# A fourth set of single row transfers per head, in place of one gather, in a graph attention and product-key attention kernel

## The chip, the cores and the metric

One NeuronCore of one Trainium2 chip. The metric is the device time of one execution in microseconds. The engines are called PE (TensorE), DVE (VectorE), ACT (ScalarE), POOL (GpSimd) and SP (SyncE); DMAs are issued by SP, ACT and POOL.

## The reference, cut to what matters

```python
def reference(x, adj, W, a, Wq_pk, pk_keys, Wq, keys_table, values_table, Wo):
    x = x + gnn(layernorm(x), adj, W, a)          # 8 batches, 1024 tokens, 128 features
    return x + ffn(layernorm(x), ...)

def ffn(x, ...):                                   # 8 heads
    q = (x @ Wq).reshape(b, n, 8, 128) * 128 ** -0.5
    kv_scores, ind = product_keys(x, Wq_pk, pk_keys)   # 16 rows of 16384 for each token and head
    k = einsum('bnhk,bnhkd->bnhd', kv_scores, keys_table[ind])
    v = einsum('bnhk,bnhkd->bnhd', kv_scores, values_table[ind])
    sim = where(causal, einsum('bihd,bjhd->bhij', q, k), neg)
    return einsum('bhij,bjhd->bhid', softmax(sim), v)... @ Wo
```

For each of 8 x 1024 tokens and each of 8 heads, 16 table rows (a key and a value side by side, 1 KB) are fetched by an index that the kernel computes, weighted and summed. That is 1,048,576 rows of 1 KB.

## The kernel before, in words

The work is cut into 64 heads (8 batches of 8 heads, numbered n = 0 to 63) of 8 units each. A unit is a tile of 128 tokens, t = 0 to 7. The table rows of a unit are 16 slots, k = 0 to 15, of 128 rows each.

**POOL** (L344 to L363) fetches them: one indirect DMA, a gather of 128 rows, for each slot, into a ring of four units (`ring`, RING = 4). Ahead of unit (n, t) it waits for the indices of that unit (`idx_ready`) and for the sum of the unit four before (`rows_summed`).

**DVE** (`head`, L1063) goes through the units in order. In unit t of head n it starts the choice of indices for unit t of head n + 1 (`choose_sets`), waits for the gathered rows of (n, t) (L1081), weights and adds slots 8 to 15 (`add_row`, L908; L917 is the first row, L920 the others) between the steps of the choice, adds PE's share of the sum (`sum_rows`, L931), and writes the indices of (n + 1, t) (`choose_rows`, L994, its last instruction L1006). So the indices of a unit are known a whole head before its rows are summed. At t = 4 the graph part writes the accumulator of the next batch (`graph_out`, L890, after the wait of L889 for the output stores of the batch before last), at t = 5 it normalises a row tile of the next batch (`graph_norm`, L903). Between batches `projection` (L822) comes in between.

**PE** weighs slots 0 to 7 (`weigh`, L646), and does the attention of the unit before. **ACT** (`head`, L515) makes the diagonals, the exponentials and the copies for it, in a fixed order written out by hand.

**The far sets.** In three units of each head, t in SETS = (3, 7, 0), slot 15 isn't gathered (L345): its 128 rows come as 128 single transfers of 1 KB each into `far`, from heads 1 on. DVE reads slot 15 from there (L912 to L915, which waits for all 128 and clears the semaphore). For this, DVE writes the 128 byte addresses (`far_at`, L1004), and a small DMA turns them into one row (`far_row`), from which the issuing engine loads addresses into registers, 32 at a time on SP, and issues the transfers (L293 on SP, L483 on ACT).

- SP serves the sets of units 3 and 7 (FAR): 256 singles a head. `far_begin(n, i)` (L273) waits for the indices and issues the small DMA; `far_fetch(n, i)` (L280) waits for it to land and for the buffer to be free (`rows_summed` of the same unit a head before), then issues four blocks of 32. `far_sets` (L298) begins set i + 1 (or set 0 of the next head) and only then fetches set i.
- ACT serves the set of unit 0 (NEAR): `near_begin` (L463) at t = 1, and `near_fetch` (L470) at the end of units 1 to 7, with 20, 20, 20, 20, 16, 16 and 16 singles.

SP also issues the load of x for the batch after next (`load`, L266, waits for L903 of the last row tile) and the 8 output stores of a batch (`stores`, L257, L264, each waits for DVE's last addition of its tile). `turn` (L306) puts the stores between the two sets of the next batch's first head.

```python
SETS = FAR + (NEAR,)
for k in range(TOPK if first or t not in SETS else FAR_ROW):
    pool.indirect_dma_start(
```

Of the kernel before, what the change touches and what calls it, by code (L numbers as in the profile page):

```python
# [11 lines left out]
U8 = mybir.dt.uint8  # L12
AX_X = mybir.AxisListType.X

P = 128
BATCH = 8
N = 1024
TILES = N // P
HEADS = 8
# [4 lines left out]
KV_BYTES = 4 * KV  # L24
# [5 lines left out]
EDGE = 256  # L30
LEAD = 2
SUMMED = UNITS - LEAD
FAR = (3, 7)
NEAR = 0
NEAR_ROWS = (0, 20, 20, 20, 20, 16, 16, 16)
SETS = FAR + (NEAR,)
FAR_ROW = TOPK - 1
LOADED = 32
BIG = 1e30
# [7 lines left out]
def gat_and_product_key_attention(nc, x, adj, W, WT, a, WqpkT, keysT, Wq, table, Wo, out):  # L47
    with ExitStack() as ctx:
# [196 lines left out]
        @block.sync  # L245
        def _(sp):
            sp.dma_start(xin[:], x[0].rearrange("(t p) d -> p t d", p=P)).then_inc(x_dma, 16)
            sp.dma_start(w_t[:], WT).then_inc(w_dma, 16)
            sp.dma_start(a_sb[:], a).then_inc(w_dma, 16)
            sp.dma_start(w_ext[:, 0:P], W).then_inc(w_dma, 16)  # L250
            sp.dma_start(mask[:].bitcast(I32), adj.rearrange("(t p) n -> p t n", p=P)).then_inc(adj_dma, 16)
            sp.dma_start(wpk_t, WqpkT).then_inc(in_dma, 16)
            sp.dma_start(keys_t, keysT).then_inc(in_dma, 16)
            sp.dma_start(wq[:], Wq.rearrange("p (h n) -> p h n", h=HEADS)).then_inc(in_dma, 16)
            sp.dma_start(wo[:], Wo.rearrange("(h p) n -> p h n", p=P)).then_inc(in_dma, 16)

            def stores(b):  # L257
                for t in range(TILES):

                    sp.wait_ge(y_added, b * HEADS * UNITS + (HEADS - 1) * UNITS + t + 1)  # L260
                    sp.sem_inc(sp_mark, 1)
                    src = acc[:, bass.ds(b % 2, 1), t * P:(t + 1) * P].rearrange("p o n -> p (o n)")
                    dst_ = out[bass.ds(b, 1), t * P:(t + 1) * P, :].rearrange("o p n -> (o p) n")
                    sp.dma_start(dst_, src).then_inc(out_dma, 16)  # L264

            def load(b):  # L266

                sp.wait_ge(g_xn, b * TILES)
                sp.sem_inc(sp_mark, 1)
                sp.dma_start(xin[:], x[bass.ds(b, 1)].rearrange("o (t p) d -> (o p) t d", p=P)) \  # L270
                    .then_inc(x_dma, 16)

            def far_begin(n, i):  # L273

                sp.wait_ge(idx_ready, n * UNITS + SETS[i] + 1)
                sp.sem_inc(sp_mark, 1)
                with nc.allow_non_contiguous_dma(reason="one table address of each token"):
                    sp.dma_start(far_row[0:1, i, :], far_at[:, i:i + 1]).then_inc(far_row_dma[i], 16)

            def far_fetch(n, i):  # L280

                sp.wait_ge(far_row_dma[i], n * 16)
                sp.sem_inc(sp_mark, 1)
                if not (isinstance(n, int) and n == 1):
                    sp.wait_ge(rows_summed, (n - 1) * UNITS + SETS[i] + 1)
                    sp.sem_inc(sp_mark, 1)
                for q in range(0, P, LOADED):
                    _, at = nc.values_load_multi_w_load_instructions(
                        far_row[0:1, i, q:q + LOADED], engines=[mybir.EngineType.SP],
                        min_val=0, max_val=(HEADS * NUM_KV - 1) * KV_BYTES,  # L290
                        skip_runtime_bounds_check_because="made of two positions below 128 and a head below 8")
                    for j in range(LOADED):
                        sp.dma_start(far[q + j:q + j + 1, i, :].bitcast(U8), table_bytes[bass.ds(at[j], KV_BYTES)]) \  # L293
                            .then_inc(far_dma[i], 16)

            last_set = len(FAR) - 1

            def far_sets(n, sets, final=False):  # L298
                for i in sets:
                    if i < last_set:  # L300
                        far_begin(n, i + 1)
                    elif not final:
                        far_begin(n + 1, 0)
                    far_fetch(n, i)

            def turn(b):  # L306
                far_sets((b + 1) * HEADS, range(0, last_set))
                stores(b)
                far_sets((b + 1) * HEADS, range(last_set, last_set + 1))

            load(1)
            far_begin(1, last_set + 1)
            far_begin(1, 0)
            far_fetch(1, last_set + 1)
            with sp.Fori(1, HEADS) as h:
                far_sets(h, range(len(FAR)))
            with sp.Fori(0, BATCH - 2) as b:
                load(b + 2)
                turn(b)
                with sp.Fori(1, HEADS) as h:  # L320
                    far_sets((b + 1) * HEADS + h, range(len(FAR)))
            turn(BATCH - 2)
            with sp.Fori(1, HEADS - 1) as h:
                far_sets((BATCH - 1) * HEADS + h, range(len(FAR)))
            far_sets(BATCH * HEADS - 1, range(len(FAR)), True)
            stores(BATCH - 1)
            sp.wait_ge(out_dma, BATCH * TILES * 16)

# [38 lines left out]
        def _(act):  # L367
# [99 lines left out]
                with nc.allow_non_contiguous_dma(reason="one table address of each token"):  # L467
                    act.dma_start(far_row[0:1, near, :], far_at[:, near:near + 1]).then_inc(far_row_dma[near], 16)

            def near_fetch(n, part):  # L470

                if NEAR_ROWS[part - 1] == 0:
                    act.wait_ge(far_row_dma[near], n * 16)
                    act.sem_inc(act_mark, 1)
                    act.wait_ge(rows_summed, (n - 1) * UNITS + NEAR + 1)
                    act.sem_inc(act_mark, 1)
                q = sum(NEAR_ROWS[:part])
                _, at = nc.values_load_multi_w_load_instructions(
                    far_row[0:1, near, q:q + NEAR_ROWS[part]], engines=[mybir.EngineType.Activation],
                    min_val=0, max_val=(HEADS * NUM_KV - 1) * KV_BYTES,  # L480
                    skip_runtime_bounds_check_because="made of two positions below 128 and a head below 8")
                for j in range(NEAR_ROWS[part]):
                    act.dma_start(far[q + j:q + j + 1, near, :].bitcast(U8), table_bytes[bass.ds(at[j], KV_BYTES)]) \  # L483
                        .then_inc(far_dma[near], 16)

            act.wait_ge(aux_mm, 1)
            nc.scalar.copy(w_ext[:, P:P + 1], wh_ps[:, 0:1]).then_inc(aux_copied, 1)
# [27 lines left out]
            def head(b, h, n, graph, ahead, first=False):  # L515
                if ahead and not first:
                    query_weights((h + 1) % HEADS, n + 1)
                for t in range(UNITS):
                    g = n + TILES
                    behind = (n, t - 1) if t else (n - 1, UNITS - 1)  # L520
                    if graph and t == 4:
                        graph_elu(g)
                    if graph and t == 5:
                        graph_sqrt(g)
                    if t or not first:
                        attend_exp(*behind)
                    if graph and t == 6:
                        graph_keep(b + 1, h, g)
                    if ahead and t == 1 and not first:
                        near_begin(n + 1)  # L530
                    if ahead:
                        t1 = (t + 1) % UNITS
                        n1 = n + 1 + (t + 1) // UNITS
                        choose_begin(n1 // HEADS if graph else BATCH - 1, n1 * UNITS + t1, t1)
                    if t or not first:
                        attend_turned(*behind)
                    if ahead:
                        choose_softmax((n + 1) * UNITS + t)
                    attend_begin(n, t)
                    if t < UNITS - 1:  # L540
                        if not first or t + 1 > SUMMED:
                            diagonals(n, t + 1)
                    elif ahead:
                        diagonals(n + 1, 0)
                    if t or not first:
                        attend_out(*behind)
                    if ahead:
                        choose_query((n + 1) * UNITS + t, t)
                    if graph and t == 1:
                        graph_exp(g)  # L550
                    if graph and t == 2:
                        graph_copy(g)
                    if ahead and t >= 1 and not first:
                        near_fetch(n + 1, t)
                if not ahead:
                    attend_exp(n, UNITS - 1)
                    attend_turned(n, UNITS - 1)
                    attend_out(n, UNITS - 1)
# [593 lines left out]
```

## Time and profile before

| What | us |
|---|---|
| median of 3 runs | 15304.31 (15302.25 to 15309.95) |
| profiled execution, first to last instruction of the core (the span) | 10159.7 |
| POOL busy in it | 7625.7 (75%) |
| DVE busy | 6962.0 (69%) |
| PE busy | 5615.2 (55%) |
| ACT busy | 3117.0 (31%) |

The page gives the profiled execution's span and no other time of it. The median of the runs is 5144.6 us above that span. Busy time does not count instructions that issue DMAs on SP and ACT, register and semaphore instructions. In the timeline views SPq and ACTq are the sequencers of SP and ACT, where DMAs are issued.

### The profile page before, as it was taken

The numbers are of one execution on the slowest core, as the hardware profiler recorded it, in microseconds if no ns is written. First come the engines' busy times: TensorE is split into PE (matmuls) and PEld (weight loads), VectorE is DVE, ScalarE is ACT, GpSimd is POOL, SyncE is SP. The second block draws the span as 40 slices with busy tenths as digits, with TensorE's granted clock in tenths as the row PEclk, the third lists the DMA queues.
The fourth block names the chain that finished last, engine by engine and source line by source line (L and its number), as shares of the span: only waits on it lengthen the run. The fifth ranks groups of instructions, "written<-read, shape, count | busy, mean of one in ns | idle before, by whom it ended". The sixth has DMA issues, their size and how long they took to land.

```text
span 10159.7 us, 173542 instructions
## 1 busy us (share of the span) xinstructions
PE 5615.2 (55%) x23108; PEld 4511.4 (44%) x23108; DVE 6962.0 (69%) x42780; ACT 3117.0 (31%) x9770; POOL 7625.7 (75%) x8020
## 2 busy tenths in 40 slices
PE   5655555555555555555555555555555555555555
PEld 4544444444444444444444444444444444444444
DVE  8866667666666667666776666766667676666663
ACT  4333233332333333333333233333333333322222
POOL 5777777777777777777777777777777777777776
PEclk7777777777777777777777777777777777777777
DMA  3333333333333333333333333333333333333333
GB/s 109 104 108 108 108 112 108 108 108 108 112 108 107 108 108 112 108 108 108 108 112 108 108 108 108 112 108 108 107 110 110 108 108 108 108 110 108 108 108 99
DMA packets 481297, 1099.25 MB, mean 108 GB/s; under 512 B 180864, under 2 KB 222720, under 8 KB 479968
## 3 DMA queue, kind: packets, MB, share of 16 engines
q0 software_dynamic: 384144, 1049.48, 36.1%
q1 hardware_dynamic: 71152, 31.60, 1.2%
q10 hardware_dynamic: 24800, 8.19, 0.4%
q14 instruction: 1184, 9.70, 0.3%
q8 instruction: 17, 0.28, 0.0%
HBM read 1084.36 MB, written 4.19 MB: 107 GB/s over the span
## 4 chain that ended last, share of the span: by engine, by line
POOL 73%; issue 24%; DVE 2%; PE 1%; POOLq 0%; DMA 0%; ACT 0%; ACTq 0%; SPq 0%; DVEq 0%
POOL ring L346 73%; DVE hot L998 0%; PE ps_o L709 0%; DMA wo<-in_Wo 0%; DVE ps_v L920 0%; POOLq L362 0%; PE ps_p L595 0%; POOLq L360 0%; DMA ring<-in_table,idx 0%; PE ps_p L599 0%; ACTq L483 0%; PE ps_s L681 0%; DVE nmax L1049 0%; PE ps_w L656 0%; DVE edge L849 0%
## 5 line engine op out<-in xcount | busy, mean ns | idle before, releaser
L346 POOL DMA_INDIRECT ring<-in_table,idx x8003 | 7624.1, 953 | 2507.7 <-issue 2440.8
L656 PE MATMUL ps_w<-ring,diag 128*128 128x256 f32 x8192 | 1996.2, 400 | 9.7 <-DMA ring<-in_table,idx 9.6
L700 PE MATMUL ps_p<-ident,prob 128*128 128x128 f32 x2304 | 548.8, 390 | 2576.1 <-ACT prob L446 2568.1
L656 PEld LDWEIGHTS ps_w<-ring,diag 128*128 128x128 f32 x8192 | 1630.3, 205 | 244.8 <-issue 12.7
L917 DVE TENSOR_SCALAR ps_v<-ring,wgt 128x256 f32<-128x256 f32 x512 | 248.7, 486 | 2147.8 <-DMA ring<-in_table,idx 2147.8
L998 DVE SCALAR_TENSOR_TENSOR hot<-rank,posf,cand 128x54 f32<-128x54 f32 x8192 | 1655.4, 270 | 0.3
L700 PEld LDWEIGHTS ps_p<-ident,prob 128*128 128x128 f32 x2304 | 371.4, 194 | 2769.7 <-ACT prob L446 1734.0
L920 DVE SCALAR_TENSOR_TENSOR ps_v<-ring,wgt,ps_v 128x256 f32<-128x256 f32 x3072 | 1478.1, 481 | 19.6
L437 ACT ACTIVATE diag<-ident,wgt 128x128 f32<-128x128 f32 x4096 | 1251.9, 391 | 0.0
L668 PE MATMUL ps_t<-ident,kv 128*128 128x128 f32 x512 | 234.4, 458 | 1642.4 <-DVE kv L931 1642.4
L709 PEld LDWEIGHTS ps_o<-probT,kv 128*128 128x128 f32 x4608 | 1040.8, 318 | 145.9 <-ACT probT L454 69.9
L446 ACT ACTIVATE prob<-ps_s,nmax 128x128 f32<-128x128 f32 (+7 forms) x512 | 378.1, 738 | 2324.8 <-issue 1777.3
L709 PE MATMUL ps_o<-probT,kv 128*128 128x128 f32 x4608 | 1035.4, 404 | 43.7 <-ACT probT L454 43.7
L668 PEld LDWEIGHTS ps_t<-ident,kv 128*128 128x128 f32 x512 | 92.1, 180 | 1803.4 <-DVE kv L931 1802.7
L681 PE MATMUL ps_s<-kT,qT 128*128 128x512 f32 (+3 forms) x1536 | 784.6, 630 | 1.6 <-issue 1.2
L998 DVE DVE_READ_ACCUMULATOR hot<-rank,posf,cand 128x1 f32 x8192 | 651.3, 79 | 0.0
L634 PE MATMUL ps_v<-pk,xt 128*128 (+1 forms) x1026 | 545.6, 632 | 13.6 <-ACT xt L412 7.5
L931 DVE TENSOR_TENSOR kv<-part,ps_w 128x256 f32<-128x256 f32 x512 | 215.7, 421 | 453.9 <-PE ps_o L709 407.0
L454 ACT COPY probT<-ps_p 128x512 f32<-128x512 f32 (+3 forms) x768 | 351.7, 480 | 414.2 <-PE ps_p L700 412.3
L681 PEld LDWEIGHTS ps_s<-kT,qT 128*128 128x128 f32 x1536 | 366.7, 271 | 194.9 <-issue 188.2
L441 ACT COPY kT<-ps_t 128x128 f32<-128x128 f32 x512 | 135.9, 265 | 977.6 <-PE ps_t L668 977.4
L941 DVE MAX8 side<-ps_v 128x8 f32<-128x128 f32 x1024 | 253.6, 289 | 212.2 <-issue 181.0
(119 smaller groups left out, 8053.9 us busy)
## 6 DMA issues: line engine op xcount, KB each, us to landing
far<-in_table SPq DMA_DIRECT2D x16256, 1.0 KB
ring<-in_table,idx POOLq DMA_INDIRECT x8003
far<-in_table ACTq DMA_DIRECT2D x7936, 1.0 KB
xin<-in_x SPq DMA_DIRECT2D x8, 512.0 KB, 4.6
mask<-in_adj SPq DMA_DIRECT2D x1, 4096.0 KB, 14.6
out_x<-acc SPq DMA_DIRECT2D x64, 64.0 KB
far_row<-far_at SPq DMA_DIRECT2D x127, 0.5 KB
far_row<-far_at ACTq DMA_DIRECT2D x62, 0.5 KB
```

The lines of the kernel that those rows point to most:

```text
L346: pool.indirect_dma_start(out=ring[:, t % RING, k, :], out_offset=None, in_=table, in_offset=bass.IndirectOffsetOnAxis(ap=idx[:, t, k:k + ...
L437: nc.scalar.mul(diag[:, k, :], ident[:], wgt[:, t, k:k + 1]).then_inc(diag_ready, 1)
L446: nc.scalar.activation(prob[:, 0:cols], ps_s[:, 0:cols], ACT.Exp, bias=nmax[:, 0:1], accum_out=psum_row[:, 0:1]).then_inc(p_exp, 1)
L454: nc.scalar.copy(probT[:, c * 512:c * 512 + m], ps_p[:, c, 0:m]).then_inc(p_copied, 1)
L634: nc.tensor.matmul(ps_sim, xt[:, t % 2, :], pk[:, bass.ds(h, 1), :, :].rearrange("p o s n -> p (o s n)"), start=True, stop=True).then_inc( ...
L656: ins = nc.tensor.matmul(pw_ps, diag[:, k, :], ring[:, t % RING, k, :], start=(k == 0), stop=(k == PE_ROWS - 1))
L668: nc.tensor.transpose(ps_t[:, 0, :], kv[:, t, 0:P], ident[:]).then_inc(k_tp, 1)
L681: nc.tensor.matmul(ps_s[:, c * 512:c * 512 + m], q, kT[:, c * 512:c * 512 + m], start=True, stop=(c < HALVES[t] - 1))
L700: ins = nc.tensor.transpose(ps_p[:, c, (j % 4) * P:(j % 4 + 1) * P], prob[:, j * P:(j + 1) * P], ident[:])
L709: ins = nc.tensor.matmul(oT_ps, kv[:, j, P:KV], probT[:, j * P:(j + 1) * P], start=(j == 0), stop=(j == t))
L920: row_sum[0] = step(nc.vector.scalar_tensor_tensor(out=part[:] if k == TOPK - 1 else ps_part, in0=rows, scalar=w, in1=ps_part, op0=ALU.mul ...
L998: c = step(nc.vector.scalar_tensor_tensor(out=hot[:, k, :], in0=rank[:], scalar=posf[:, k:k + 1], in1=cand[:, 1, :], op0=ALU.is_equal, op1 ...
```

## The change

A fourth set is added. The units with a set become SETS = (1, 3, 6, 0), so POOL gathers 124 slots a head in place of 125. SP issues the sets of units 3 and 6 and rows 32 to 127 of the set of unit 1 (352 singles a head); ACT issues the set of unit 0 and rows 0 to 31 of the set of unit 1 (160 singles a head). ACT's parts at the end of units 1 to 7 become 28, 28, 24, 24, 24 (set of unit 0), 16 and 16 (set of unit 1).

`far_fetch` now issues the `far_begin` of the next set ahead of its own last block of 32, and not ahead of all four. The stores of a batch move there too, ahead of the last block of the third set of the next batch's first head. Before the first head, SP fetches the set of unit 0 and begins that of unit 1 within it.

```diff
-FAR = (3, 7)
+FAR = (1, 3, 6)
 NEAR = 0
-NEAR_ROWS = (0, 20, 20, 20, 20, 16, 16, 16)
+SHARED = 0
 SETS = FAR + (NEAR,)
+ACT_ROWS = (32, 0, 0, P)
+NEAR_PLAN = {1: ((3, 0, 28),), 2: ((3, 28, 56),), 3: ((3, 56, 80),), 4: ((3, 80, 104),), 5: ((3, 104, 128),),
+             6: ((0, 0, 16),), 7: ((0, 16, 32),)}
...
-            def far_fetch(n, i):
+            def far_fetch(n, i, first, after_begin=None, follow=None):
...
-                for q in range(0, P, LOADED):
+                for q in range(first, P, LOADED):
+                    if q == P - LOADED:
+                        if follow is not None:
+                            far_begin(*follow)
+                        if after_begin is not None:
+                            stores(after_begin)
...
-            def far_sets(n, sets, final=False):
-                for i in sets:
+            def far_sets(n, final=False, stored=None):
+                for i in range(len(FAR)):
                     if i < last_set:
-                        far_begin(n, i + 1)
-                    elif not final:
-                        far_begin(n + 1, 0)
-                    far_fetch(n, i)
-
-            def turn(b):
-                far_sets((b + 1) * HEADS, range(0, last_set))
-                stores(b)
-                far_sets((b + 1) * HEADS, range(last_set, last_set + 1))
+                        far_fetch(n, i, ACT_ROWS[i], follow=(n, i + 1))
+                    else:
+                        far_fetch(n, i, ACT_ROWS[i], stored, None if final else (n + 1, 0))
 
             load(1)
             far_begin(1, last_set + 1)
-            far_begin(1, 0)
-            far_fetch(1, last_set + 1)
+            far_fetch(1, last_set + 1, 0, follow=(1, 0))
...
             with sp.Fori(0, BATCH - 2) as b:
                 load(b + 2)
-                turn(b)
+                far_sets((b + 1) * HEADS, stored=b)
...
-            def near_fetch(n, part):
+            def near_fetch(n, i, first, stop):
...
-                if NEAR_ROWS[part - 1] == 0:
-                    act.wait_ge(far_row_dma[near], n * 16)
+                if first == 0:
+                    act.wait_ge(far_row_dma[i], n * 16)
                     act.sem_inc(act_mark, 1)
-                    act.wait_ge(rows_summed, (n - 1) * UNITS + NEAR + 1)
-                    act.sem_inc(act_mark, 1)
+                    if not (isinstance(n, int) and n == 1):
+                        act.wait_ge(rows_summed, (n - 1) * UNITS + SETS[i] + 1)
+                        act.sem_inc(act_mark, 1)
...
-                    if ahead and t >= 1 and not first:
-                        near_fetch(n + 1, t)
+                    if ahead:
+                        for i, lo, hi in NEAR_PLAN.get(t, ()):
+                            if i == SHARED or not first:
+                                near_fetch(n + 1, i, lo, hi)
```

## Rows read from the trace of the kernel before

**Rows 1.** The page: span, and busy time, share and instructions of each engine.

```profile
span 10159.7 us, 173542 instructions
PE 5615.2 (55%) x23108; PEld 4511.4 (44%) x23108; DVE 6962.0 (69%) x42780; ACT 3117.0 (31%) x9770; POOL 7625.7 (75%) x8020
```

**Rows 2.** The page: the chain that ended last, shares by line (first line of two).

```profile
POOL 73%; issue 24%; DVE 2%; PE 1%; POOLq 0%; DMA 0%; ACT 0%; ACTq 0%; SPq 0%; DVEq 0%
```

**Rows 3.** Waits of POOL, whole span: us in total, times, longest.

```profile
POOL ring L346 <- issue: 2440.8, 7998, 0.3
POOL ring L346 <- DVE idx L1006: 55.8, 1, 55.8
POOL ring L346 <- DVE kv L931: 11.1, 4, 10.2
```

**Rows 4.** The page's costliest group: busy us, mean ns, idle before.

```profile
L346 POOL DMA_INDIRECT ring<-in_table,idx x8003 | 7624.1, 953 | 2507.7 <-issue 2440.8
```

**Rows 5.** Waits of all engines, those of DVE on rows: us, times, longest.

```profile
DVE ps_v L917 <- DMA ring<-in_table,idx: 2147.8, 420, 10.4
...
DVE part L920 <- DMA far<-in_table: 9.0, 2, 7.0
```

**Rows 6.** Timeline of SP at a batch boundary: start us, length us, what.

```profile
5036.72 0.48 SPq L278 DMA_DIRECT2D far_row<-far_at  x1
5039.66 48.33 SPq L293 DMA_DIRECT2D far<-in_table  x128
5091.09 0.41 SPq L270 DMA_DIRECT2D xin<-in_x  x1
...
5168.39 5.88 SPq L264 DMA_DIRECT2D out_x<-acc  x8
```

**Rows 7.** Waits of SP, whole span: us in total, times, longest.

```profile
SPq L276 <- DVE idx L1006: 3170.9, 126, 32.4
```

**Rows 8.** Timeline of DVE, ten moments; L1006 ends the index choice of a unit.

```profile
5076.76 0.35 DVE L903 TENSOR_SCALAR xn<-x,gmv,row 128x128 f32<-128x128 f32 x1
...
5151.96 0.42 DVE L931 TENSOR_TENSOR kv<-part,ps_w 128x256 f32<-128x256 f32 x1 [8.92 <-PE ps_o L709]
...
5172.86 0.26 DVE L1006 CAST idx<-idxf 128x16 uint32<-128x16 f32 x1
...
5214.89 0.26 DVE L890 TENSOR_SCALAR acc<-x 128x128 f32 x1
...
5254.66 0.17 DVE L1006 CAST idx<-idxf 128x16 uint32<-128x16 f32 x1
...
5316.46 0.27 DVE L1006 CAST idx<-idxf 128x16 uint32<-128x16 f32 x1
...
5350.86 0.15 DVE L1004 TENSOR_SCALAR far_at<-idxf 128x1 uint32<-128x1 f32 x1
5350.93 0.17 DVE L1006 CAST idx<-idxf 128x16 uint32<-128x16 f32 x1
...
5412.30 0.17 DVE L1006 CAST idx<-idxf 128x16 uint32<-128x16 f32 x1
...
5473.70 0.19 DVE L1006 CAST idx<-idxf 128x16 uint32<-128x16 f32 x1
```

**Rows 9.** Timeline of ACT, end of unit 1 of head 33 and after it.

```profile
5318.84 6.50 ACTq L483 DMA_DIRECT2D far<-in_table  x20
5325.38 0.47 ACT L446 ACTIVATE prob<-ps_s,nmax 128x256 f32<-128x256 f32 x1 [7.06 <-issue]
```

**Rows 10.** Timeline of POOL: the first gather of unit 4 of head 32.

```profile
5183.46 0.95 POOL L346 DMA_INDIRECT ring<-in_table,idx  x1 [0.31 <-issue]
```

**Rows 11.** Timeline of SP at the start: the first set 0 and set 3.

```profile
240.72 49.04 SPq L293 DMA_DIRECT2D far<-in_table  x128
...
293.05 48.56 SPq L293 DMA_DIRECT2D far<-in_table  x128
```

**Rows 12.** Timeline of POOL: its one long stall behind DVE, head 1, unit 2.

```profile
269.69 0.97 POOL L346 DMA_INDIRECT ring<-in_table,idx  x1 [10.15 <-DVE kv L931]
```

More of the change, by code:

```diff
@@ L296, in _ @@
             last_set = len(FAR) - 1
-            def far_sets(n, sets, final=False):
-                for i in sets:
+            def far_sets(n, final=False, stored=None):
+                for i in range(len(FAR)):
                     if i < last_set:
-                        far_begin(n, i + 1)
-                    elif not final:
-                        far_begin(n + 1, 0)
-                    far_fetch(n, i)
-            def turn(b):
-                far_sets((b + 1) * HEADS, range(0, last_set))
-                stores(b)
-                far_sets((b + 1) * HEADS, range(last_set, last_set + 1))
+                        far_fetch(n, i, ACT_ROWS[i], follow=(n, i + 1))
+                    else:
+                        far_fetch(n, i, ACT_ROWS[i], stored, None if final else (n + 1, 0))
             load(1)
             far_begin(1, last_set + 1)
-            far_begin(1, 0)
-            far_fetch(1, last_set + 1)
+            far_fetch(1, last_set + 1, 0, follow=(1, 0))
             with sp.Fori(1, HEADS) as h:
-                far_sets(h, range(len(FAR)))
+                far_sets(h)
             with sp.Fori(0, BATCH - 2) as b:
                 load(b + 2)
-                turn(b)
+                far_sets((b + 1) * HEADS, stored=b)
                 with sp.Fori(1, HEADS) as h:
-                    far_sets((b + 1) * HEADS + h, range(len(FAR)))
-            turn(BATCH - 2)
+                    far_sets((b + 1) * HEADS + h)
+            far_sets((BATCH - 1) * HEADS, stored=BATCH - 2)
             with sp.Fori(1, HEADS - 1) as h:
-                far_sets((BATCH - 1) * HEADS + h, range(len(FAR)))
-            far_sets(BATCH * HEADS - 1, range(len(FAR)), True)
+                far_sets((BATCH - 1) * HEADS + h)
+            far_sets(BATCH * HEADS - 1, True)
             stores(BATCH - 1)
@@ L468, in near_begin @@
                     act.dma_start(far_row[0:1, near, :], far_at[:, near:near + 1]).then_inc(far_row_dma[near], 16)
-            def near_fetch(n, part):
-                if NEAR_ROWS[part - 1] == 0:
-                    act.wait_ge(far_row_dma[near], n * 16)
+            def near_fetch(n, i, first, stop):
+                if first == 0:
+                    act.wait_ge(far_row_dma[i], n * 16)
                     act.sem_inc(act_mark, 1)
-                    act.wait_ge(rows_summed, (n - 1) * UNITS + NEAR + 1)
-                    act.sem_inc(act_mark, 1)
-                q = sum(NEAR_ROWS[:part])
+                    if not (isinstance(n, int) and n == 1):
+                        act.wait_ge(rows_summed, (n - 1) * UNITS + SETS[i] + 1)
+                        act.sem_inc(act_mark, 1)
                 _, at = nc.values_load_multi_w_load_instructions(
-                    far_row[0:1, near, q:q + NEAR_ROWS[part]], engines=[mybir.EngineType.Activation],
+                    far_row[0:1, i, first:stop], engines=[mybir.EngineType.Activation],
                     min_val=0, max_val=(HEADS * NUM_KV - 1) * KV_BYTES,
                     skip_runtime_bounds_check_because="made of two positions below 128 and a head below 8")
-                for j in range(NEAR_ROWS[part]):
-                    act.dma_start(far[q + j:q + j + 1, near, :].bitcast(U8), table_bytes[bass.ds(at[j], KV_BYTES)]) \
-                        .then_inc(far_dma[near], 16)
+                for j in range(first, stop):
+                    act.dma_start(far[j:j + 1, i, :].bitcast(U8), table_bytes[bass.ds(at[j - first], KV_BYTES)]) \
+                        .then_inc(far_dma[i], 16)
             act.wait_ge(aux_mm, 1)
```

## The prediction

> **What bounds the kernel now.** I read first who ends last. In the chain of the whole span POOL's gathers and the "issue" time between them are 97% [rows 2]. Busy shares alone would not say this: POOL is at 75% and DVE at 69% [rows 1]. The waits of POOL settle it [rows 3]. Nearly all its idle time, 2440.8 us in 7998 pieces of 0.3 us, is the gap from one gather to the next, on which nothing but POOL itself works. For indices it waits once, at the start (55.8 us), and for DVE to free the ring 11.1 us in all. So POOL runs from gather to gather without a stop, and a gather costs its busy time and the gap: (7624.1 + 2440.8) / 8003 = 1.258 us [rows 4]. 8003 of them are 10065 of the 10159.7 us.
>
> Everything else has to be no more than in time. DVE waits 2147.8 us for gathered rows, in 420 of 512 units, and only 9.0 us, at the start, for single transfers [rows 5]. SP stands 3170.9 us waiting for indices [rows 7], 50 us of a head's 157.
>
> **The change, part by part.** *Removed:* one gather in each of heads 1 to 63, 125 to 124, 63 in all: 8003 become 7940. Each is worth 1.258 us as long as POOL never waits. One is lost again: in head 1 POOL stands 10.15 us at unit 2, until DVE has summed unit 6 of head 0 [rows 12]. It comes there one gather earlier now and waits that much longer. That leaves 62 x 1.258 = 78.0 us.
>
> *SP: 256 to 352 singles a head.* A set of 128 takes 48.33 us from first to last issue and 2.46 us ahead of it (from the end of L278 to the first single: landing of the small DMA, loading of addresses) [rows 6], so 12.7 us for a block of 32. Eleven blocks are 140 us, three begins at 0.48 us make 141. A head takes 157.2 us now (5316.46 to 5473.70, unit 1 to unit 1 [rows 8]) and 156.0 then. SP is filled to 91%, and 15 us are left. Its waits for indices, with index 1 of head n + 1 ready at time 0: the last block of the set of unit 6 goes out to 13; three blocks of set 1 to 51, whose last needs index 3, ready at 34.5; set 3 has three blocks out at 90, then waits for index 6 until 95.8, and ends at 109; set 6 has three blocks out at 147 and waits for the next index 1 at 156. DVE reads these sets at about 156, 190 and 252: over 80 us to spare for each. In steady state this costs nothing, and what hides it is that a set is asked for a head ahead.
>
> *The batch boundary,* where `load` now holds set 1 and not set 3. `load` waits for L903 at 5076.76 [rows 8]. From 5077.5, SP needs ten blocks without a stop until its last block of set 6: 5077.5 + 127 + 1 = 5206. Set 1 is out at 5116, set 3 at 5167; unit 1 of head 32 ends at 5172.86. Then come the stores, 5.88 us [rows 6], to 5212, and the last block to 5225, against 5254.66 for unit 6. All arrive. The tight one is L890 at 5214.89, which waits until the stores of two batches before the one it writes have landed. They are issued at 5168 to 5174 before and to about 5212 then, so 3 us are left for landing, and I count a DVE stall of 0 to 5 us at each of six boundaries. DVE lags most here, yet the sum of unit 0 of head 32 at 5151.96 is 31 us ahead of the gather that needs it, at 5183.46 [rows 8, 10]. The stall stands in front of units where DVE waits for rows anyway. Counted at 0, upper end 6 x 5 = 30 us.
>
> *The start.* SP's first set comes 30 us earlier, since its begin of the second set no longer waits ahead of it (240.72 becomes about 210 [rows 11]). Then follow without a stop four blocks of set 0, three of set 1 and four of set 3, so set 3 ends near 210 + 11 x 12.7 = 350, where it ended at 341.6 (293.05 + 48.56), and set 6 near 400. DVE may wait some 10 us for each in head 1 and up to 20 us in head 2; POOL is three units, over 55 us, from needing those sums. Zero, upper end 20 us.
>
> *ACT: 128 to 160 singles a head.* 20 of them take 6.50 us, and the `prob` behind them stood 7.06 us [rows 9], 0.353 us each. Units 1 and 2 take 28, so 2.8 us more, units 3 and 4 four more, unit 5 eight more; what moves into units 6 and 7 is as many as before. That is 11.3 us a head. Queued behind it are `prob` and PE's transposes of the unit before, then the scores that DVE's maximum needs. DVE's cover is its own wait for rows, 2147.8 / 64 = 34 us a head [rows 5]. Zero on the path. ACT also waits at unit 6 for the small DMA of set 1, which SP issues at index 1, five units earlier; at a boundary at 5194 against about 5255. No stop.
>
> *DVE:* one more address column a head, 0.15 us [rows 8], under the same cover. *POOL's own rate:* the same transfers leave its queue and go to two others. Nothing in the rows prices a slower gather beside more singles; by the gap that is constant at 0.30 us while SP and ACT issue, I take no change, and 0.2% of the gathers' 10065 us (20 us) to either side.
>
> **Sum.** Span 10159.7 - 78.0 = 10081.7 us. The median of the runs is 5144.6 us above the span, which no row covers; the three runs lie within 7.7 us of each other, so I take it as a constant around the kernel: 15304.3 - 78.0 = 15226.3 us, 0.51% less. About 0.2% (31 us) is what a measurement of this kernel can tell from no change.
>
> The Trainium skill speaks against this change (DMA: Bandwidth & Descriptors, Rules for kernel authors): many small transfers should be made into one large one, since under 64 KB one pays mostly overhead. The trace agrees on the overhead, 48.33 us of issue for what a gather does in 1.258. By that rule taken as a cost on the path the sum would be 63 x (48 - 1.3) = some 2900 us slower; by the rows it lies on SP and ACT, which do not end last.
>
> **Rivals.** *(a) The part outside the span scales.* If the timed executions are longer throughout by 15304.3 / 10159.7 = 1.506, each gather is worth 1.89 us and the result is 15304.3 - 117.5 = 15187. For it: a constant of 5 ms is odd. Against: nothing in the trace shows a slower gather. 11%. The Trainium skill (Runtime: NRT & Kernel Launch, The ~15us preamble/postamble breakdown) puts 9 to 15 us around a kernel; no run shows that here, and it would leave the 5 ms inside the execution, which speaks for (a).
>
> *(b) Partly given back:* boundary stores and the start reach POOL, up to 30 + 20 us: 15240 to 15276. Against: 31 us and 55 us of ring in hand. 9%.
>
> *(c) Slower: SP becomes the bound.* Its place is the eleven blocks a head. At over 156.0 / 11 = 14.2 us a block SP falls behind, and above 14.3 us the kernel is slower than before, 12% more than the 12.7 us of now. If a single cost what an output store costs to issue (5.88 / 8 = 0.74 us, the nearest dearer row [rows 6]) in place of 0.38, the head would be 352 x 0.74 = 259 us and the kernel 6 ms slower; a third of that step, 0.12 us on a single, is 352 x 0.12 = 42 us, a head of 183 us and 63 x 26 = 1640 us slower: 16940. Against: the three sets shown, at the start and in the middle, took 48.33, 48.56 and 49.04 us [rows 6, 11], which differ by 1.5%. 8%.
>
> *(d) The gather stays, or something else cancels it:* within 31 us of before. Slots are left out by `t in SETS`, so it does go. 4%.
>
> **How the numbers follow.** Forecast 68%, (a) 11%, (b) 9%, (c) 8%, (d) 4%. The range takes in the forecast with its 20 us on the gather's rate, (a) and (b): 15180 to 15275; outside are (c) and (d), 12%, and the ends of the others. Faster by over 0.2%: 68 + 11 + 8 = 87%. Within: 5%. Slower: 8%.
>
> **What would show it.** Right: 7940 gathers at 1.258 us, POOL still waiting for no one but in head 1, a span near 10082, SP's waits for indices down from 50 to some 15 us a head, DVE's wait for singles still near zero. Wrong: POOL waiting for L931 in every head (c), or at every eighth (b); mean gather or gap longer; a time that falls by 1.5 times the fall of the span (a).

## The result, and the profile after

| | before | after | after / before (95%) |
|---|---|---|---|
| median of 4 runs, us | 15306.77 | 17009.96 | 1.1113 (1.11 to 1.1126) |
| span of the profiled execution, us | 10159.7 | 17004.4 | |

The kernel after is 11% slower; 15226 was forecast, with 15180 to 15275 as the range. The profiled execution after took 17006.56 us, 2.2 us more than its span. So nothing of 5144 us lies around this kernel, and the profile of before shows an execution that is unlike the timed ones. The page of the kernel after, against [rows 1, 2]:

```profile
span 17004.4 us, 190424 instructions
PE 5905.6 (35%) x23108; PEld 4760.9 (28%) x23108; DVE 7154.1 (42%) x42844; ACT 3064.3 (18%) x9770; POOL 7557.6 (44%) x7957
...
SPq 62%; issue 37%; DVE 1%; another core or an unknown queue 0%; PE 0%; ACT 0%; DMA 0%; DVEq 0%; ACTq 0%
SPq L301 52%; SPq L296 8%; SPq L281 1%; SPq L267 0%; DVE hot L1001 0%; DMA wo<-in_Wo 0%; DVE ps_v L923 0%; SPq L289 0%; SPq L288 0%; SPq L286 0%; ACT L398 0%; DVE edge L852 0%; DVE edge L865 0%; SPq L278 0%
...
L347 POOL DMA_INDIRECT ring<-in_table,idx x7940 | 7556.1, 952 | 9371.7 <-issue 6604.2
```

The reader is to see who took POOL's place. The engines are busy for about as long as before, within a span that is two thirds longer, and the chain is SP's queue: L301 issues the singles, L296 loads their addresses. A gather still takes 952 ns (953 in [rows 4]). POOL's idle time is now pauses between the gathers of one unit and the next: 510 of them last over 1 us, 7050 us together, and the profile of before has one of 10 us. The mean granted clock of TensorE is lower too, 0.650 against 0.728, but PE is busy only 290 us longer in a span that is 6845 us longer, and DVE's additions of gathered rows (L923, L920 before) keep their 481 ns, so a slower clock isn't what costs. The waits of POOL, and those of DVE for singles, in the kernel after, against [rows 3, 5]:

```profile
POOL ring L347 <- issue: 6604.2, 7743, 40.1
POOL ring L347 <- DVE kv L934: 2647.3, 187, 44.2
...
DVE part L923 <- DMA far<-in_table: 1454.3, 121, 49.0
```

The timeline of SP in the kernel after, one head, against [rows 6]:

```profile
8022.60 67.72 SPq L301 DMA_DIRECT2D far<-in_table  x96
8090.53 0.51 SPq L281 DMA_DIRECT2D far_row<-far_at  x1
8093.53 91.43 SPq L301 DMA_DIRECT2D far<-in_table  x128
8185.16 0.49 SPq L281 DMA_DIRECT2D far_row<-far_at  x1
8188.12 94.95 SPq L301 DMA_DIRECT2D far<-in_table  x128
8283.29 0.49 SPq L281 DMA_DIRECT2D far_row<-far_at  x1
```

128 singles take 91 to 95 us where they took 48.33, and a head 263.6 us (8022.60 to 8286.23, where the next head's first set starts). SP never waits for an index but once. What stretches its issue is seen when the issues are held against POOL's. The instructions of L301 in the kernel after, first in 18 us in which POOL gathers without a pause, then in 7 us in which it rests (count; ns min/median/max):

```profile
L301 SPq DMA_DIRECT2D far<-in_table x14: 3/14/702, 8365.6 to 8383.4; - x14
L301 SPq MOVE far<-in_table x13: 4/15/700, 8366.3 to 8382.6; - x13
```

```profile
L301 SPq MOVE far<-in_table x22: 13/29/29, 8386.9 to 8393.6; - x22
L301 SPq DMA_DIRECT2D far<-in_table x22: 218/225/321, 8386.9 to 8393.7; - x22
```

The timeline of POOL for the same stretch of the kernel after:

```profile
8364.23 0.99 POOL L347 DMA_INDIRECT ring<-in_table,idx  x1 [18.97 <-issue]
8365.52 0.95 POOL L347 DMA_INDIRECT ring<-in_table,idx  x1 [0.30 <-issue]
...
8383.32 0.94 POOL L347 DMA_INDIRECT ring<-in_table,idx  x1 [0.30 <-issue]
8393.97 1.00 POOL L347 DMA_INDIRECT ring<-in_table,idx  x1 [9.71 <-issue]
```

14 singles in 18 us, 1.3 us each, against 0.32 us each while POOL rests. Some DMA instructions stretch to 0.7 us, and so do some plain register MOVEs; the others are recorded as short as 3 ns, so the pace says more here than the length of one instruction. Over the whole trace SP's singles start 1.20 us apart on average while POOL gathers and 0.43 us apart in its pauses, the loading of addresses between the blocks included (pairs less than 5 us apart, a pause being one of over 1 us). In the profile of before it is 0.38 us while POOL gathers. In the first profile of the kernel before SP issued at full pace while POOL gathered without a pause [rows 3, 6].

### The profile page after: what moved, and what is told of

Its sections match the earlier page's. It is cut to its first block, busy times and chain, and to the rows that moved or that the text cites. A ratio compares the mean times of both kernels' runs of the same rounds, so it can differ in the third digit from the quotient of the medians.

```text
span 17004.4 us, 190424 instructions
## 1 busy us (share of the span) xinstructions
PE 5905.6 (35%) x23108; PEld 4760.9 (28%) x23108; DVE 7154.1 (42%) x42844; ACT 3064.3 (18%) x9770; POOL 7557.6 (44%) x7957
## 4 chain that ended last, share of the span: by engine, by line
SPq 62%; issue 37%; DVE 1%; another core or an unknown queue 0%; PE 0%; ACT 0%; DMA 0%; DVEq 0%; ACTq 0%
SPq L301 52%; SPq L296 8%; SPq L281 1%; SPq L267 0%; DVE hot L1001 0%; DMA wo<-in_Wo 0%; DVE ps_v L923 0%; SPq L289 0%; SPq L288 0%; SPq L286 0%; ACT L398 0%; DVE edge L852 0%; DVE edge L865 0%; SPq L278 0%
## 5 line engine op out<-in xcount | busy, mean ns | idle before, releaser
L659 PE MATMUL ps_w<-ring,diag 128*128 128x256 f32 x8192 | 2313.9, 446 | 6.9 <-issue 6.8
L659 PEld LDWEIGHTS ps_w<-ring,diag 128*128 128x128 f32 x8192 | 1866.8, 234 | 337.2 <-issue 18.5
L923 DVE SCALAR_TENSOR_TENSOR ps_v<-ring,wgt,ps_v 128x256 f32<-128x256 f32 x3072 | 1476.4, 481 | 444.4 <-remote 276.1
L1063 DVE SCALAR_TENSOR_TENSOR acc<-ps_o,rz,acc 128x128 f32 (+1 forms) x512 | 179.4, 350 | 1742.1 <-remote 1271.9
L718 PE MATMUL ps_o<-wo,oT 128*128 (+1 forms) x1024 | 308.7, 394 | 1439.5 <-ACT oT L459 795.5
L923 DVE SCALAR_TENSOR_TENSOR part<-far,wgt,ps_v 128x256 f32<-128x256 f32 x252 | 121.0, 480 | 1454.4 <-DMA far<-in_table 1454.3
L718 PEld LDWEIGHTS ps_o<-wo,oT 128*128 128x128 f32 x1024 | 205.1, 250 | 1505.2 <-ACT oT L459 768.4
L1016 DVE TENSOR_SCALAR wgt<-ew,ewsum 128x16 f32<-128x16 f32 x512 | 127.9, 250 | 1170.8 <-remote 899.0
L955 DVE MATCH_VALUE_LOAD sidx<-side,left 128x8 f32 x1024 | 88.0, 86 | 1182.4 <-remote 839.2
L419 ACT ACTIVATE qT<-ps_t 128x128 f32<-128x128 f32 x512 | 142.2, 278 | 2263.3 <-remote 1922.4
```

Of the source, the lines that this page charges most:

```text
L659: ins = nc.tensor.matmul(pw_ps, diag[:, k, :], ring[:, t % RING, k, :], start=(k == 0), stop=(k == PE_ROWS - 1))
L718: nc.tensor.matmul(y_ps, oT[:], wo[:, bass.ds(h, 1), :].rearrange("p o n -> p (o n)"), start=True, stop=True).then_inc(y_mm, 1)
L923: row_sum[0] = step(nc.vector.scalar_tensor_tensor(out=part[:] if k == TOPK - 1 else ps_part, in0=rows, scalar=w, in1=ps_part, op0=ALU.mul ...
```

## The experiments

Each set of runs has the kernel before timed on the same chip. The ratios below are against it.

**First set: is the time in the kernel, and what do single sets do?** e1 is the kernel before. e2 has no singles:

```diff
-FAR = (3, 7)
+FAR = ()
-SETS = FAR + (NEAR,)
+SETS = ()
```

with the calls of `far_begin`, `far_fetch`, `near_begin` and `near_fetch` left out. e3 keeps the set of unit 0 (`FAR = ()`), e4 those of units 3 and 7 (`SETS = FAR`).

> The kernel before, unchanged, profiled again, with 256 single transfers a head on SP and 128 on ACT. Theory S (stalled issue): in the kernel after, SP and ACT issue singles at 0.32 us while POOL gathers nothing, and in steps of 0.7, 1.4 and 2.1 us while it gathers; the timed runs of the kernel before were in that state too and its first profile was not. Then this profile shows a span near 15300 us, POOL's gaps no longer at 0.30 us, and SPq L293 issues of 0.70 us. Rival C (a constant outside the span): span near 10160 us and a time near 15305 us.

> All 16 slots of all units are gathered, no single transfers: 64 x 128 = 8192 gathers. Theory S: nothing stalls, POOL runs from gather to gather at 1.258 us, 8192 x 1.258 = 10306, span and time near 10390 us, a third less than the kernel before. Rival C: span 10400, time 15540 us. Rival T (gathers themselves are slower in timed runs, 1.9 us each): time near 15650 us.

> Only the set of unit 0 stays, 128 singles a head on ACT (127 gathers removed to 127 a head, 8129 in all). Theory S with the singles' number deciding: each single that meets a gather costs its engine about 1.7 us; 128 of them on ACT are over 200 us a head, so some 11000 to 14000 us. If both engines issuing at once is what starts the stalls: near 10310 us.

> Only the sets of units 3 and 7 stay, 256 singles a head on SP (126 gathers a head, 8066 in all). If the stall needs only one engine's singles beside gathers: SP is as slow as in the kernel before, 15000 us or a little less. If it takes SP and ACT at once: near 10230 us.

Measured: the kernel before 10138.26 us, e1 10137.73 with a span of 10135.2, e2 10364.53 (ratio 1.0223, 1.0194 to 1.0253), e3 10288.34 (1.0148), e4 10207.27 (1.0067). Neither theory's line for e1 came out: the span is near 10160 and the time is too. This chip runs the kernel before a third faster than the chip of the first comparison. I call such a chip quick and the other kind stalling. The constant outside the span is dead. Here each set of singles is a gain: 76 us from e2 to e3, 150 more from e3 to the kernel before with two more sets, or 75 to 76 a set, and 69 us from e4 to the kernel before; 63 gathers at 1.258 us would be 79. e3 and e4 met no stall and say nothing of it. For e1 on this chip, L293:

```profile
L293 SPq MOVE far<-in_table x16256: 29/29/42, 241.9 to 10067.6; - x199
L293 SPq DMA_DIRECT2D far<-in_table x16256: 224/225/457, 242.0 to 10067.6; - x199
```

**Second set: the kernel after again (e5), and without singles (e6).** The kernels are unchanged.

> The kernel after, unchanged. The kernel before took 15307 us in the first comparison and 10138 us in the runs of e1, so the stall depends on where or when a program runs, and a comparison is only good within one set of runs. Theory S: where the kernel before is at 10138 us, the singles go out at 0.32 us each beside gathers, and the kernel after is 62 gathers of 1.258 us faster, 10060 us; where before is at 15307, after is at 17010. Rival N (the larger number of singles is what starts the stall): after is near 17000 us in either case.

> The kernel without singles (8192 gathers), unchanged from e2, where it took 10364.5 us. Theory S: it has nothing that can stall, so it takes 10365 us also where the kernel before takes 15307 us; then it is the fastest of the three there. If the chip state slows the gathers too: far over 10400 us there.

Measured: before 15566.48, e5 17358.16 (1.1151, 1.1133 to 1.117), e6 13617.13 (0.8747, 0.8729 to 0.8764). A stalling chip. The kernel after repeats its 11%. The kernel without singles is the fastest of the three here, but my 10365 us for it was wrong by 3250: the stall isn't of singles alone. The page of e6, then its waits of DVE:

```profile
DVE 57%; another core or an unknown queue 26%; issue 9%; PE 6%; ACT 1%; DVEq 1%; DMA 0%; ACTq 0%; SPq 0%
...
L336 POOL DMA_INDIRECT ring<-in_table,idx x8192 | 7789.0, 951 | 5780.6 <-issue 4407.8
```

```profile
DVE top L962 <- remote: 1563.9, 413, 5.8
...
DVE side L941 <- DVE sidx L938: 106.3, 182, 1.1
```

Gathers take 951 ns here too (949 in e2). But DVE, between two of its own instructions (L938 and L941, the second waits for the first's semaphore), stands 0.58 us on average in 182 cases, and 1563.9 us ahead of L962; in e2 neither wait exists. SP's few register MOVEs last up to 728 ns in e6 and at most 42 in e2. So other engines are held up without any singles, DVE becomes the one that ends last (57% of the chain), and POOL pauses over 1 us 509 times, each time ahead of the first gather of a unit.

**Third set: which part of the change?** e7 is the kernel before, e8 the kernel after. e9 is the kernel after without its fourth set, so that only the new order of begins, stores and ACT's parts is left (125 gathers, 256 and 128 singles):

```diff
-FAR = (1, 3, 6)
+FAR = (3, 6)
-ACT_ROWS = (32, 0, 0, P)
+ACT_ROWS = (0, 0, P)
```

with ACT's parts at units 1 to 5 alone. e10 moves 64 more singles from SP to ACT:

```diff
-ACT_ROWS = (32, 0, 0, P)
+ACT_ROWS = (96, 0, 0, P)
-             6: ((0, 0, 16),), 7: ((0, 16, 32),)}
+             6: ((0, 0, 32),), 7: ((0, 32, 64), (0, 64, 96))}
```

> The kernel before, once more, for its profile beside the next three on one chip. Two conditions have been seen: one in which it takes 10138 us (call it quick) and one in which it takes 15307 to 15566 (stalling). Theory S for the stalling one: while POOL gathers, about half of the singles on SP last 0.7 us in place of 0.23, and none while POOL rests; POOL gathers at 1.258 us in both and rests 80 us a head. Rival D: the DMA queues are full, then packets start later after their issue than the 1.08 us of the quick profile.

> The kernel after. In the quick condition theory S says that the sum of the prediction holds there: 62 gathers of 1.258 us, 78 us faster than the kernel before, 10060 us, POOL not waiting. In the stalling condition 11% slower than before, as in the first comparison and in e5. Rival N (352 singles are too many for SP in any condition): slower than 10138 in the quick one too.

> The kernel after without its fourth set: sets of units 3, 6 and 0, 256 singles on SP and 128 on ACT, 125 gathers a head, with the new order of begins, stores and ACT parts. Quick: 10138 us, the same as before within 0.1%. Stalling: theory S says that the 128 added singles are what costs, so it is at or below the kernel before, 15300 to 15600 (the new order takes 5 us of exposed waits a head off SP, so up to 2% less). Rival O (the new order of waits is what costs): near 17000 to 17360, as after.

> The kernel after with 64 more singles of the fourth set on ACT: SP 288 and ACT 224 a head (ACT at units 6 and 7). Quick: POOL does not wait, 10060 us as after. Stalling: if SP's issue is the bound (62% of the chain of the kernel after is SP's queue), 64 singles less at 0.75 us shorten a head by up to 48 us, so 14300 to 16000 us; rival L (the sum of all engines' stalls binds, not SP's): within 2% of after, or slower.

Measured, a quick chip again: before 10158.63, e7 10158.33, **e8 10082.49 (0.9925, 0.9908 to 0.9941), 76.1 us faster**, e9 10155.22 (0.9996), e10 10988.29 (1.0817). Rival N is out: 352 singles a head are not too many for SP where nothing stalls. The profile of e8 is the one that the prediction described, by its page, the waits of POOL and of DVE on the sets, and the waits of SP:

```profile
span 10083.2 us, 190424 instructions
...
POOL 72%; issue 24%; DVE 1%; PE 1%; ACTq 1%; POOLq 0%; DMA 0%; ACT 0%; SPq 0%; DVEq 0%
...
L347 POOL DMA_INDIRECT ring<-in_table,idx x7940 | 7560.0, 952 | 2494.7 <-issue 2424.5
```

```profile
POOL ring L347 <- DVE kv L934: 13.4, 2, 13.1
...
DVE part L923 <- DMA far<-in_table: 6.3, 2, 4.1
```

```profile
SPq L272 <- DVE xn L906: 473.1, 7, 170.3
SPq L279 <- DVE idx L1009: 248.3, 33, 28.4
SPq L264 <- DVE acc L1063: 120.9, 7, 20.2
```

The expectation for e10 missed by 900 us. The chain of e10 by its page, then waits of PE, ACT and DVE:

```profile
ACTq 41%; PE 28%; issue 16%; DVE 10%; ACT 4%; POOL 1%; DMA 0%; DVEq 0%; SPq 0%; POOLq 0%
```

```profile
PE ps_p L703 <- ACT prob L447: 4845.2, 491, 28.0
...
ACT L430 <- issue: 1175.8, 42, 28.4
...
DVE kv L934 <- PE ps_o L712: 1789.1, 63, 31.4
```

ACT stands up to 28.4 us ahead of the first instruction of a head, behind 64 singles in one burst at unit 7. PE's attention waits for it, and DVE's sum of the next head's first unit, which must wait for the last output sum (63 times, once a head), for PE. With 224 singles ACT is the bound even where nothing stalls.

**Fourth set: the same four questions where it stalls.** e11 is the kernel before, e12 the kernel of e9, e13 that of e10, e14 that of e4.

> The kernel before, for its profile in the stalling condition if the chip shows it (time 15300 to 15570 us; in the quick one 10140 to 10160, as in e1 and e7, and nothing new). Theory S, stalling: SP's queue ends last or nearly so, 40 to 55% of the singles that SP issues while POOL gathers last over 0.6 us, none while POOL rests, POOL rests some 80 us a head.

> The kernel after without its fourth set (256 singles on SP, 128 on ACT, 125 gathers), new order kept. Quick: 10155 us as in e9. Stalling: theory S (the number of singles costs) puts it at or up to 2% below the kernel before; rival O (the new order costs) at 17000 us or more.

> The kernel after with 64 more singles on ACT (SP 288, ACT 224). Quick: 10988 us as in e10, where ACT is what is late. Stalling: if SP's queue is the bound of the kernel after, 64 x 0.75 = 48 us a head less on SP, as far as ACT lets it: 14300 to 16500 us. If not SP's queue but the stalls of all engines bind: 17000 us or more.

> Sets of units 3 and 7 on SP alone (256 singles a head on SP, none on ACT). Quick: 10207 us as in e4. Stalling: without singles it was 13617 us (e6) and with all three sets 15566. If singles on SP stall by POOL's gathers alone: SP needs as long as in the kernel before, 15000 to 15570 us. If they stall by ACT's singles beside them: near 13600 us.

Measured, a stalling chip: before 15286.68, e11 15287.45, e12 15191.89 (0.9932, 0.9916 to 0.9948), e13 16902.16 (1.1055, 1.1022 to 1.1088), e14 14606.92 (0.9554, 0.9526 to 0.9581). Three things follow. The new order is not what costs, it is a gain of 0.7% here and nothing on a quick chip: rival O is out and the fourth set's singles are the cause. The stalls don't need both queues: with singles on SP alone the chain of e14 is SP's queue. But e14 met neither of its expectations (15000 to 15570, or near 13600): it lies between them, and ACT's 128 singles cost as well. And e13 missed its 14300 to 16500: with 64 singles fewer SP is no longer the bound, but ACT is next, as in e10. For e11, L293 over the whole span; then the first lines of the chains of e11, e12, e14 and e13, in this order:

```profile
L293 SPq MOVE far<-in_table x16256: 2/29/1479, 331.0 to 15285.9; - x199
L293 SPq DMA_DIRECT2D far<-in_table x16256: 3/225/1482, 331.1 to 15285.9; - x199
```

```profile
issue 24%; another core or an unknown queue 23%; DVE 16%; SPq 11%; ACTq 11%; PE 8%; ACT 6%; DVEq 0%; DMA 0%
```

```profile
another core or an unknown queue 30%; issue 21%; ACTq 16%; DVE 14%; PE 10%; ACT 9%; DVEq 0%; DMA 0%; SPq 0%
```

```profile
SPq 56%; issue 42%; DVE 1%; PE 0%; another core or an unknown queue 0%; ACT 0%; DMA 0%; DVEq 0%; ACTq 0%
```

```profile
another core or an unknown queue 28%; ACTq 27%; issue 20%; ACT 9%; DVE 9%; PE 7%; DVEq 0%; DMA 0%; SPq 0%
```

The kernel before, when it is timed on such a chip, is no longer POOL's. Its chain goes through all engines; SP still waits 261.3 us for indices. Theory S had SP's queue last or nearly so in e11, and that was wrong: it is 11% of the chain. Of its other signs the 84 us a head of POOL's pauses came out; of SP's singles 35% last over 0.6 us while POOL gathers, where 40 to 55% were expected, and 4% while it rests. A register MOVE of SP lasts up to 1479 ns in e11 and at most 42 in e1, the same program. Rival D, full DMA queues, has little for it: the packet of a single starts 0.84 us (median) after its issue in e11, sooner than the 1.08 us of e7, and at most 4 are issued and not started (5 in e7). These delays are rough in e11: with singles and packets matched in order, 22% of the packets start before the recorded start of their own issue (none in e7), so on such a chip part of the instructions are recorded late. The pace doesn't hang on those records: while POOL gathers, the packets themselves start 1.11 us apart on average in e11 and 0.38 in e7.

**Fifth set: does SP's count decide?** e15 puts ACT's 32 singles of the fourth set on SP (`ACT_ROWS = (0, 0, 0, P)`), e16 is the kernel after.

> The kernel after with its fourth set whole on SP: SP 384 singles a head, ACT 128. Quick condition: twelve blocks at 12.9 us and the waits for indices fill 156 us or pass it, so SP is the bound or just not: 10080 to 10500 us. Stalling: if SP's queue bounds the kernel after, 32 singles more at 0.75 us are 24 us a head, some 1500 us slower than after, 18500 us; as only a single issued while POOL rests is added (0.33 us), at least 10 us a head, 650 us slower. If the stalls of all engines bind and not SP, within 2% of the kernel after.

> The kernel after, as the reference of e15 on the same chip. Theory S: 0.9925 of the kernel before if that takes 10140 to 10160 us, 1.11 if that takes 15290 to 15570.

Measured, a stalling chip: before 15519.93, e15 18146.54 (1.1695, 1.1656 to 1.1733), e16 17276.09 (1.1134, 1.1097 to 1.117). The chain of e15:

```profile
SPq 63%; issue 36%; DVE 1%; another core or an unknown queue 0%; PE 0%; ACT 0%; DMA 0%; DVEq 0%; ACTq 0%
```

32 singles more on SP, taken from ACT, are 870 us, over 63 heads 13.8 us a head or 0.43 us a single. That lies between the 10 and the 24 us a head expected, and the rival, within 2% of the kernel after, is out. From e14 (256 on SP) to e16 (352) it is (1.1134 - 0.9554) x 15520 / 63 / 96 = 0.41 us a single, over two chips. In these three kernels the chain is SP's queue, and SP's count sets the time. In the others it doesn't: e12 has the 256 singles of e14 on SP and 128 more on ACT, takes 585 us longer, and SP isn't in its chain. So that both steps have the same price assumes that ACT's singles cost nothing once SP ends last, which no run shows by itself. The price is less than the mean of 0.75 us a single in the kernel after, since the added time is time in which POOL rests: its pauses over 1 us are 7333.5 us in e16 and 8201.1 in e15, 867.6 of the 870 us, and in these pauses the singles of e16 start 0.43 us apart.

All sets together, by kind of chip (the kernel before = 1):

| kernel | singles a head, SP + ACT | quick chips | stalling chips |
|---|---|---|---|
| no singles | 0 | 1.0223 | 0.8747 |
| sets of units 3, 7 | 256 + 0 | 1.0067 | 0.9554 |
| before | 256 + 128 | 1 (10138, 10159 us) | 1 (15287 to 15566 us) |
| new order, no fourth set | 256 + 128 | 0.9996 | 0.9932 |
| after | 352 + 160 | 0.9925 | 1.1113, 1.1151, 1.1134 |
| 64 more on ACT | 288 + 224 | 1.0817 | 1.1055 |
| all on SP | 384 + 128 | not run | 1.1695 |

No kernel tried is the best on both. The new order without the fourth set is nowhere slower than before.

## Why the prediction was wrong

- **The step that failed: "I take it as a constant around the kernel".** The sum had a term of 5144.6 us that no row covered, and carried it over. In each profiled execution since, the time is about 2 us over the span: 17006.56 and 17004.4, 10364.92 and 10363.1. The profile of before was of an execution of the quick kind, the runs beside it of the stalling kind. So every cover was read in the wrong condition, and a gap of a third of the time was itself the sign of it. Carrying the gap over doesn't by itself make the kernel slower; what does is the next step, read in that wrong condition.
- **"SP is filled to 91%, and 15 us are left."** Right for a quick chip: e8 has SP waiting, without the first 170.3 us, 303 + 248 + 121 = 672 us or 11 us a head. On a stalling one a block of 32 costs 94.6 / 4 = 23.6 us (8093.53 to 8188.12) in place of 12.7, and a head 263.6 us in place of 156: SP's 141 us a head is the term that turned the gain into a loss, and "in steady state this costs nothing" the path that it had wrong there.
- **Rival (c)** named what happened, SP's eleven blocks above 14.2 us, with the "against" that three sets differed by 1.5%; all three were of one execution. Its price, 1640 us, is near the 1703 measured by chance: SP loses far more, but the kernel it is compared with stalls too. The dearer case that it worked out and set aside, 259 us a head and 6 ms, is the one that came, 263.6 us a head and 6.8 ms over the span of before; its price was borrowed from the output stores, so that is luck as well. 8% was too low with 5 ms unexplained.
- **Rival (a)** had the timed executions longer throughout, as they are, but put it on the gathers. They take 949 to 954 ns on either kind of chip; POOL's pauses grow.
- **"62 x 1.258 = 78.0 us".** Right where nothing stalls: 76.1 us between medians on one chip, a span of 10083.2 against 10081.7, (7560.0 + 2424.5) / 7940 = 1.2575 us a gather, and a stall in head 1 of 13.1 us where 10.15 + 1.26 = 11.4 was forecast.
- **The start, the boundary, ACT's cover.** On the quick chip all held at zero: DVE waits 6.3 us for singles, and 0.4 us for the stores ahead of L893, once. On the stalling one the boundary's stall is 230.6 us in 6 times, behind SP.
- The Trainium skill (DMA: Bandwidth & Descriptors, Rules for kernel authors) speaks against many small transfers. On the quick chip the trace disagrees: the kernel after is 0.75% faster, as the overhead lies on queues with room. Where it stalls, the trace agrees: the kernel without singles is 12.5% faster than the kernel before. The Trainium skill (Runtime: NRT & Kernel Launch, The ~15us preamble/postamble breakdown) puts 9 to 15 us around a kernel. No run here shows that figure, only the 2 us between time and span, and both spoke against my constant of 5144.6 us.

## What to carry to other kernels

Hold the span of the profile against the times before anything else; where they differ by far more than the 2 us of these runs, the profile shows another behaviour than the one that is timed, and no cover read from it counts. When work moves from one long instruction on GpSimd to hundreds of short ones on other sequencers, ask for the price of an instruction while GpSimd gathers, on more than one chip: here it was 0.32 us a single or 1.3. And a comparison holds for its kind of chip: this change is 0.75% faster on one and 11% slower on another.

## What the runs showed of the hardware that I had not expected

Of the chips whose identity the runs give, two ran the kernel before in 10138 and 10159 us and three in 15287 to 15566, each alike over its runs. Each chip was used on one occasion only, so whether it is the chip or the occasion that makes the difference is not shown; "quick chip" and "stalling chip" are names for what was seen.

On the slower three, while GpSimd issues indirect DMAs, SP's singles start 1.19 to 1.28 us apart on average in place of 0.38 to 0.39, and ACT's 0.62 to 0.92 in place of 0.32 to 0.34. In the kernel after 35% of SP's DMA issues then last over 0.6 us, nearly all of these 0.65 to 0.75 us and a few twice that, in place of 0.23, and register MOVEs stretch likewise in place of 0.03. A wait of DVE on its own semaphore takes 0.58 us in place of none. The gathers themselves (949 to 954 ns) and DVE's additions of gathered rows (480 to 484 ns) are as fast as elsewhere. When GpSimd pauses, the others are back at full pace within some 2.3 us: 99% of the long instructions that SP starts in a pause of the kernel after start before that.

What makes a chip of one kind or the other was not found: no experiment could set it. That the pause of GpSimd is what ends the stall is read from the traces. They do not tell GpSimd's own work from the packets of its gathers, the last of which end 1.5 us after it in the kernel after, and a kernel with singles and without any gathers wasn't tried. Nor was it tried whether the recording of the instructions has a part in the stall.
